# Every edge-value multiply of a two-layer GNN kernel reads its edge values from PSUM

## The chip, the cores and the metric

One NeuronCore of a Trainium2 chip runs the whole program. The metric is the device time of one execution in microseconds (us).

## The reference

Two graph layers over 6250 nodes with 96 features and 106250 edges that are sorted by destination, each followed by a residual and a layer norm:

```python
h = gelu(x @ W_pre + b_pre)
msg = h[src] * edge_attr                      # layer 0: gather, multiply
aggr = segment_sum(msg, dst)
x1 = x + aggr;  y = gelu(gelu(x1 @ W1 + b1) @ W2 + b2)
x2 = layernorm(x + (x1 + y))
deg = segment_sum(1, dst); dinv = rsqrt(max(deg, 1))
h2 = x2 @ W_lin.T + b_lin                     # layer 1
agg = segment_sum(h2[src] * dinv[src] * dinv[dst], dst)
out = layernorm(x2 + relu(agg + x2 @ W_root.T + b_root))
```

The change touches the second line only, and there the place from which VectorE reads `edge_attr`.

## The kernel before

**Units.** The edges are cut in tiles of 128 and the tiles in units of five (`UT`): units 0 to 165 are whole, unit 166 holds the last ten edges. For each unit GpSimd gathers the five tiles of `h[src]` with five indirect DMAs into one of eight slots of `gath` (L923); SP loads the edge values into one of four slots of `edg`; VectorE makes a one-hot of each edge's destination within a window of nodes (`hot`, L1352) and multiplies gath by the edge values into `msg` (`multiply`, L1376); TensorE multiplies msg by the one-hot and so sums the messages of the unit's window in the bank `seg` or `seg_odd` (L1590); VectorE adds the finished window to `sumT` (`add`, L1396). A window is 128 nodes wide up to group 21 (units 0 to 65) and 64 from there on.

**What frees what.** The gathers of unit u wait for the multiply of unit u-8, SP's load of edge values for the multiply of unit u-4. The multiply of unit u waits for its gathers and its edge values.

**The bank.** Up to `AHEAD` = 108 every even unit (`by_bank`) has its edge values copied by ScalarE from `edg` into the PSUM bank `edges_ps` (`copy_edges`, L1086), and its multiply reads the bank; the odd units, and all from 108 on, read `edg` in SBUF. The copy waits until the last multiply that read the bank is done. The bank `edges_ps` is later the third bank for sums of pieces. The bank `counters` holds `iota_ps` (0 to 127, against which every one-hot is compared) and the two iotas of the builder in bf16.

**The second layer beside the first.** Layer 1 runs as dense counts: a builder on VectorE makes one-hots for pairs of windows (L1472, L1474, four pairs in one build, 157 builds, two buffers), TensorE turns each of the 625 pairs into counts (L1622, banks `bank_q[0]` and `bank_b`), ScalarE casts them into SBUF (L1026), SP stores them to HBM and loads them back as pieces (eight buffers), and TensorE sums pieces against the ready node rows (L1646), which VectorE adds to `sumT` or `upper` (`dense`, L1499). The node steps of layer 0 (step0, 13 chunks with up to 16 phases over all engines: gelu, norm, products) are put between them.

**The order.** `schedule()` writes one list, and each engine walks it and executes its own items in that order. One slot of the list belongs to one unit: the unit itself (on VectorE one-hot and multiply, on TensorE the sums), then adds, dense sums, stores and loads, then in at least eight places the pairs, each with a piece or a step beside it where one is due. A slot up to unit 104 holds one build with four pairs or two builds with eight. The copy for unit u+1 stands at place 2 of slot u, behind two pairs. From `AHEAD` on the multiply of unit u+1 already stands in slot u (`hot` at place 3, `product` at place 5).

Of the kernel before, what the change touches and what calls it, by code (L numbers as in the profile page):

```python
# [12 lines left out]
P = 128  # L13
N_NODES, D = 6250, 96
# [5 lines left out]
UT = 5  # L20
# [3 lines left out]
UNITS = BODY_TILES // UT  # L24
# [8 lines left out]
WIN = 128  # L33
# [5 lines left out]
GS, ES, MS = 8, 4, 5  # L39
# [84 lines left out]

def group_of(u):
    return min(u // GU if u < WIDE * GU else WIDE + u - WIDE * GU, GROUPS - 1)


def by_bank(u):

    return u % 2 == 0 and u < AHEAD


def reach(g):
# [40 lines left out]
def schedule():  # L175
# [68 lines left out]
    for u in range(ALL_UNITS):  # L244
        if u < AHEAD:
            order += [("add", g) for g in range(WIDE, GROUPS) if added[g] == u]
            order.append(("unit", u))
        else:
            order.append(("sums", u))
        if u >= ALL_UNITS - GS:  # L250
            order.append(("back", u - (ALL_UNITS - GS)))
        if u == FLAG_AT:
            order.append(("flag", 0))
        order += [("add", g) for g in range(WIDE) if added[g] == u]
        flush(u)
        order += [("store", k) for k in range(STORES) if stored[k] == u]
        if u >= LOAD_AT and (u - LOAD_AT) % LOAD_STEP == 0 and (u - LOAD_AT) // LOAD_STEP < len(LOADED):
            order.append(("load", LOADED[(u - LOAD_AT) // LOAD_STEP]))
        credit += CREDIT[u > built]
        pairs = []  # L260
        for j in range(BUILDS):
            if BUILD_AT + int(j * BUILD_STEP) == u:
                order.append(("build", j))
                pairs += range(j * BP, min(j * BP + BP, PAIRS))
        slots = max(len(pairs), 2 * CT)
        for i in range(slots):
            for k, (p, c) in enumerate(steps[u]):
                if k * slots // len(steps[u]) == i:
                    order.append(("step0", p, c))
                    if p == phases_of(c)[-1]:  # L270
                        known = c + 1
            if i == 2 and u < UNITS and by_bank(u + 1):
                order.append(("edges", u + 1))
            if AHEAD <= u + 1 < ALL_UNITS:
                if i == 2:
                    order += [("add", g) for g in range(WIDE, GROUPS) if added[g] == u + 1]
                if i == 3 and u <= TOGETHER:
                    order.append(("hot", u + 1))
                elif i == 5 and u < TOGETHER:
                    order.append(("product", u + 1))  # L280
                elif i == 4 and u == TOGETHER:
                    order += [("product", u + 1), ("hot", u + 2), ("product", u + 2)]
            if i < len(pairs):
                order.append(("pair", pairs[i]))
                for k in range(STORES):
                    if last_pair_of(k) == pairs[i]:
                        stored[k] = u + 1
            if credit >= CT:
                was = len(pieces)
                if open_run or not (waiting and u <= built + 1):  # L290
                    next_piece(u, next(n for until, n in LEAST if u < until))
                if len(pieces) > was:
                    credit -= tiles_of_cut(pieces[-1][1])
                else:
                    credit = min(credit, 2.0 * CT)
# [32 lines left out]
def build(nc, x, xT_in, src, dst, first, tile_first, tile_rows, edge, edge_tail, W_pre, b_pre, W1, b1, W2, b2,  # L328
          WlinT, b_lin, WrootT, b_root, out):
    with ExitStack() as ctx:  # L330
# [252 lines left out]
        one_bank = sum(1 for r in range(len(runs)) if any(  # L583
            x[2] == r and order.index(("piece", q)) < last_pair for q, x in enumerate(pieces)))

        last_copied = max(u for u in range(UNITS) if by_bank(u))
        two_banks = sum(1 for r in range(len(runs)) if any(
            x[2] == r and order.index(("piece", q)) < sums_at(last_copied + 1) for q, x in enumerate(pieces)))

# [87 lines left out]

        def set_bank(c):
            return (bank_q[0], bank_q[1], edges_ps, seg, seg_odd, bank_a, bank_b)[c % 7]

        def group_sum(g):

# [302 lines left out]
        def _(act):  # L985
# [91 lines left out]
                        act.dma_start(rows[part], back(c)[part]).then_inc(s_out[c % ZS], 16)  # L1077

            def copy_edges(u):
                if u > 0:  # L1080
                    act.wait_ge(s_msg, u - 1)
                else:
                    act.wait_ge(s_kb, 3)
                act.wait_ge(s_edge[u % ES], edges_landed(u))
                if u < UNITS:
                    act.copy(edges_ps[:, 0:UT * D], edg[:, u % ES].rearrange("p j d -> p (j d)")).then_inc(s_eps, 1)  # L1086
                else:
                    for j, k in enumerate(TAILS):
                        last = act.copy(edges_ps[0:k, j * D:(j + 1) * D], edg[0:k, u % ES, j, :])
                    last.then_inc(s_eps, 1)  # L1090

            act.wait_ge(s_w, 8 * 16)
# [23 lines left out]
        def general_dve(dve, r, rows):  # L1116

            if r == 0:
                dve.memset(sumT[:], 0.0).then_inc(s_cleared, 1)
                dve.wait_ge(s_cleared, 1)  # L1120
                dve.wait_ge(s_const, 2)
                dve.sem_inc(s_lmsg, 1)
            dve.sem_inc(s_ladd[r], 1)

            def general_unit(g, ks):
                tiles = len(ks)
                dve.wait_ge(s_ladd[r], g * WINDOWS + 1)
                dve.tensor_copy(dst_f[:, 0:tiles], dsts[:, bass.ds(g * UT, tiles)]).then_inc(s_ldst[r], 1)
                if r == 0:
                    dve.wait_ge(s_lgath[0], g * (16 * UT) + 16 * tiles)  # L1130
                    dve.wait_ge(s_ledge, g * 16 + 16 * (tiles if ks is TAILS else 1))
                    if ks is TAILS:
                        for j, rows_j in enumerate(ks):
                            last = dve.tensor_tensor(msg[0:rows_j, 0, j, 0:D], gath[0:rows_j, j, :],
                                                     edg[0:rows_j, 0, j, :], ALU.mult)
                        last.then_inc(s_lmsg, 1)
                    else:
                        dve.tensor_tensor(msg[:, 0, 0:tiles, 0:D], gath[:, 0:tiles],
                                          edg[:, 0, 0:tiles], ALU.mult).then_inc(s_lmsg, 1)
                with dve.Fori(0, WINDOWS) as w:  # L1140
                    dve.wait_ge(s_ldst[r], g + 1)
                    dve.wait_ge(s_ladd[r], g * WINDOWS + w + 1)
                    dve.tensor_scalar(rel[:, 0:tiles], dst_f[:, 0:tiles],
                                      win_start[:, bass.ds(w, 1)], None, ALU.subtract
                                      ).then_inc(s_lrel[r], 1)
                    dve.wait_ge(s_lrel[r], g * WINDOWS + w + 1)
                    dve.tensor_tensor(
                        onehot[:, 0, 0:tiles],
                        iota_ps[:].unsqueeze(1).to_broadcast([P, tiles, WIN]),
                        rel[:, 0:tiles].unsqueeze(2).to_broadcast([P, tiles, WIN]),  # L1150
                        ALU.is_equal).then_inc(s_loh[r], 1)
                    dve.wait_ge(s_lseg[r], g * WINDOWS + w + 1)
                    dve.tensor_tensor(sumT[0:rows, bass.ds(w * WIN, WIN)],
                                      sumT[0:rows, bass.ds(w * WIN, WIN)],
                                      seg[0:rows, 0:WIN], ALU.add).then_inc(s_ladd[r], 1)

            with dve.Fori(0, UNITS) as g:
                general_unit(g, sizes(0))
            general_unit(UNITS, TAILS)
            dve.wait_ge(s_ladd[r], ALL_UNITS * WINDOWS + 1)  # L1160

# [118 lines left out]
        def _(dve):  # L1280
# [65 lines left out]
            def hot(u):  # L1346
# [3 lines left out]
                w = reach(group_of(u))  # L1350
                if u < UNITS:
                    dve.tensor_tensor(  # L1352
                        onehot[:, s, :, 0:w], iota_ps[:, 0:w].unsqueeze(1).to_broadcast([P, UT, w]),
                        rel[:, u * UT:(u + 1) * UT].unsqueeze(2).to_broadcast([P, UT, w]),
                        ALU.is_equal).then_inc(s_oh, 1)
                else:
                    for j, k in enumerate(TAILS):
                        t = u * UT + j
                        last = dve.tensor_tensor(onehot[0:k, s, j, 0:w], iota_ps[0:k, 0:w],
                                                 rel[0:k, t:t + 1].to_broadcast([k, w]), ALU.is_equal)  # L1360
                    last.then_inc(s_oh, 1)

            def multiply(u):
                s = u % MS
                if by_bank(u):
                    dve.wait_ge(s_eps, u // 2 + 1)
                    edges = by_tile(edges_ps, UT)
                else:
                    dve.wait_ge(s_edge[u % ES], edges_landed(u))
                    edges = edg[:, u % ES]  # L1370
                if u < EARLY:
                    dve.wait_ge(s_h, CHUNKS - (-(u + 1) * UT // CT))
                else:
# [453 lines left out]
```

## Time and profile before

| | us |
|---|---|
| median of 3 runs | 1125.99 (1120.19 to 1127.88) |
| the profiled execution | 1126.56 |
| its span, from the first to the last instruction | 1124.8 |
| TensorE busy | 938.3 (83%) |
| GpSimd busy | 833.6 (74%) |
| VectorE busy | 719.1 (64%) |
| ScalarE busy | 473.2 (42%) |

All times of the trace are from the start of the span. Instructions that only issue or wait aren't counted as busy; idle time before an instruction is given with what ended it. Where that is "issue", the engine waited for nothing that the profile shows. The granted clock of TensorE is a share of 2.4 GHz.

### The profile page before, as it was taken

What the parts mean: (1) busy time and instruction counts of PE and PEld (TensorE: products, weight loads), DVE (VectorE), ACT (ScalarE), POOL (GpSimd) and SP (SyncE); (2) the same over time, 40 slices, a digit from 0 to 9 for tenths busy, and PEclk for the clock granted to TensorE, in tenths of its full rate; (3) what the DMA queues carried; (4) which work ended last, traced back from release to release, by engine and by line L of the source; (5) the groups of instructions that cost most, each with busy time, mean ns of one, the idle gap of its engine ahead of it and who ended that gap; (6) DMA issues with size and microseconds to landing.
All of it is one profiled execution on the core that took longest, in us unless ns stands there. A gap on an engine that the chain in (4) does not pass through costs nothing. (4 is left out here: it accounts for less than half of the span.)

```text
span 1124.8 us, 21017 instructions
## 1 busy us (share of the span) xinstructions
PE 938.3 (83%) x7410; PEld 792.9 (70%) x7847; DVE 719.1 (64%) x1521; ACT 473.2 (42%) x884; POOL 833.6 (74%) x917
## 2 busy tenths in 40 slices
PE   5877677677767887898889889899999989889786
PEld 5844445344444775685678678799999989789786
DVE  8976797677767667756576666634336454646567
ACT  1366685665665566555565556600001010001115
POOL 7877777777777777777777777777777777777715
PEclk9997986888877999696699999999999999879898
DMA  9457776675666769777788889998999997767853
GB/s 286 111 156 251 243 227 218 225 231 173 236 212 194 241 217 300 229 239 240 251 259 262 269 292 300 282 286 251 266 269 293 266 257 217 217 167 203 206 127 90
DMA packets 185723, 260.28 MB, mean 231 GB/s; under 512 B 68651, under 2 KB 163883, under 8 KB 179019
## 3 DMA queue, kind: packets, MB, share of 16 engines
q1 hardware_dynamic: 158049, 215.51, 59.7%
q0 software_dynamic: 26992, 42.82, 16.1%
q8 instruction: 61, 1.00, 0.4%
q10 hardware_dynamic: 569, 0.53, 0.2%
q14 instruction: 52, 0.42, 0.1%
HBM read 173.15 MB, written 85.62 MB: 230 GB/s over the span
## 5 line engine op out<-in xcount | busy, mean ns | idle before, releaser
L923 POOL DMA_INDIRECT gath<-table_h,srcs x806 | 784.6, 973 | 245.6 <-issue 242.5
L1646 PE MATMUL bank_q<-piece_raw,early_late 128*96 128x250 bf16 x2805 | 339.1, 273 | 8.2 <-DVE sumT L1499 6.0
L1646 PEld LDWEIGHTS bank_q<-piece_raw,early_late 128*96 128x96 bf16 x2805 | 304.9, 124 | 2.1 <-issue 0.5
L1026 ACT CAST counts_raw<-bank_q 128x490 bf16<-128x490 f32 x300 | 185.2, 617 | 201.9 <-PE bank_q L1622 198.7
L1026 ACT CAST counts_raw<-bank_b 128x490 bf16<-128x490 f32 x300 | 186.2, 621 | 46.8 <-PE bank_b L1622 46.1
L1622 PE MATMUL bank_q<-hots_raw 128*128 128x245 bf16 x626 | 134.9, 300 | 80.2 <-ACT counts_raw L1026 55.1
L1474 DVE TENSOR_TENSOR hots_raw<-counters,kb 128x1960 bf16<-128x1960 bf16 (+1 forms) x157 | 182.5, 1163 | 0.0
L1622 PE MATMUL bank_b<-hots_raw 128*128 128x245 bf16 x624 | 134.9, 301 | 19.9 <-ACT counts_raw L1026 7.1
L1590 PE MATMUL seg<-onehot,msg 128*97 128x64 f32 (+1 forms) x830 | 111.2, 290 | 23.9 <-DVE msg L1376 23.6
L1590 PE MATMUL seg_odd<-onehot,msg 128*97 128x64 f32 (+1 forms) x832 | 108.8, 286 | 23.3 <-DVE msg L1376 22.6
L1590 PEld LDWEIGHTS seg<-onehot,msg 128*97 128x97 f32 x830 | 103.2, 193 | 33.6 <-DVE msg L1376 31.6
L1472 DVE TENSOR_TENSOR hots_raw<-counters,kb 128x1024 bf16<-128x1024 bf16 (+1 forms) x157 | 106.8, 681 | 24.8 <-PE bank_b L1622 24.8
L1590 PEld LDWEIGHTS seg_odd<-onehot,msg 128*97 128x97 f32 x832 | 101.3, 189 | 29.8 <-DVE msg L1376 27.3
L1622 PEld LDWEIGHTS bank_q<-hots_raw 128*128 128x128 bf16 x626 | 44.6, 102 | 110.2 <-ACT counts_raw L1026 99.5
L1038 ACT ACTIVATE y<-bank_a,b1c 96x512 f32<-96x512 f32 (+2 forms) x14 | 8.8, 629 | 236.3 <-PE bank_a L1661 236.2
L1376 DVE TENSOR_TENSOR msg<-gath,edg 128x480 f32<-128x480 f32 x112 | 72.8, 650 | 48.6 <-DMA gath<-table_h,srcs 48.6
L1622 PEld LDWEIGHTS bank_b<-hots_raw 128*128 128x128 bf16 x624 | 50.1, 103 | 75.7 <-ACT counts_raw L1026 68.0
L1352 DVE TENSOR_TENSOR onehot<-counters,rel 128x320 f32<-128x320 f32 (+1 forms) x166 | 102.0, 614 | 0.0
L1376 DVE TENSOR_TENSOR msg<-gath,edges_ps 128x480 f32<-128x480 f32 x54 | 35.2, 652 | 81.1 <-ACT edges_ps L1086 81.0
L1499 DVE TENSOR_TENSOR sumT<-sumT,bank_q 96x250 f32<-96x250 f32 x91 | 37.1, 409 | 70.2 <-PE bank_q L1646 66.3
L1538 PEld LDWEIGHTS <-w_pre 97*128 97x128 bf16 x437 | 45.1, 109 | 51.8 <-DVE hots_raw L1474 27.0
L1646 PE MATMUL edges_ps<-piece_raw,early_late 128*96 128x250 bf16 x648 | 79.5, 273 | 0.0
(237 smaller groups left out, 796.7 us busy)
## 6 DMA issues: line engine op xcount, KB each, us to landing
counts_hbm<-counts_raw SPq DMA_DIRECT2D x50, 1531.2 KB
piece_raw<-counts_hbm SPq DMA_DIRECT2D x250, 250.0 KB
edg<-in_edge SPq DMA_DIRECT2D x166, 240.0 KB
gath<-table_h,srcs POOLq DMA_INDIRECT x806
piece_raw<-counts_hbm SPq DMA_DIRECT2D x38, 125.0 KB
piece_raw<-counts_hbm SPq DMA_DIRECT2D x25, 187.5 KB
counts_raw<-counts_hbm SPq DMA_DIRECT2D x4, 625.0 KB, 6.5
table_h<-stage SPq DMA_DIRECT2D x12, 192.0 KB, 5.4
```

What stands on the lines that cost most here:

```text
L923: pool.indirect_dma_start(gath[0:k, u % GS * UT + j, :], None, table[0], bass.IndirectOffsetOnAxis(ap=srcs[0:k, t:t + 1], axis=0)).then_in ...
L1026: act.copy(counts[:, k % 2, :, i * WD:(i + 2) * WD].rearrange("p a (w n) -> p a w n", w=2), counted).then_inc(s_kept, 1)
L1038: act.activation(y1[0:D, 0:tiles * P], bank_a[0:D, 0:tiles * P], ACT.Gelu, bias=b1c[:, 0:1]).then_inc(s_y1, 1)
L1352: dve.tensor_tensor(onehot[:, s, :, 0:w], iota_ps[:, 0:w].unsqueeze(1).to_broadcast([P, UT, w]), rel[:, u * UT:(u + 1) * UT].unsqueeze(2). ...
L1376: dve.tensor_tensor(msg[:, s, :, 0:D], gath[:, slot_tiles(u), :], edges, ALU.mult).then_inc(s_msg, 1)
L1472: dve.tensor_tensor(hot_b(j)[:, 0:n], iota_b.unsqueeze(1).to_broadcast([P, n, P, 2]), blocks.unsqueeze(2).to_broadcast([P, n, P, 2]), ALU. ...
L1474: dve.tensor_tensor(hot_k(j)[:, 0:n], iota_k.unsqueeze(1).to_broadcast([P, n, KC, 2]), keys.unsqueeze(2).to_broadcast([P, n, KC, 2]), ALU. ...
L1499: dve.tensor_tensor(total, total, run_sum, ALU.add).then_inc(s_dense, 1)
L1538: pe.ldweights(w_pre[:].bitcast(BF16)[:, 0:P])
L1590: last = pe.matmul(group_sum(g), msg[0:k, u % MS, j, :], onehot[0:k, u % MS, j, 0:reach(g)], start=(u == first_unit(g) and j == 0), stop=( ...
L1622: last = pe.matmul(pair_bank(m)[:, w * KC:(w + 1) * KC], hot_b(j)[:, i, :, w], hot_k(j)[:, i, :, w], start=True, stop=True)
L1646: mm = pe.matmul(sums(r)[0:D, 0:DN], parts[:, FINE[c] + i, part, :], rows, start=(first and i == 0 and part == 0), stop=(last and i == til ...
```

## The change

`by_bank` is gone: every unit has its edge values copied into a bank, and every multiply reads one. Up to unit 107 that is `edges_ps`; from unit 108 on it is the bank `counters`, whose place the copies overwrite, so the one-hots of these units compare against `iota` in SBUF. The copy of unit u waits for the multiply of u-1 (before, for that of u-2), the first copy into `counters` also for all builds and for the one-hots of units 0 to 107. The copy for unit u+1 stays at place 2 of slot u.

```diff
-            if i == 2 and u < UNITS and by_bank(u + 1):
+            if i == 2 and u <= TOGETHER:
                 order.append(("edges", u + 1))
+                if u == TOGETHER:
+                    order.append(("edges", u + 2))
...
-        last_copied = max(u for u in range(UNITS) if by_bank(u))
+        last_copied = AHEAD - 1
...
+        def edges_of(u):
+            return (edges_ps if u < AHEAD else counters)[:, 0:UT * D]
+        def iota_of(u):
+            return iota_ps if u < AHEAD else iota
...
             def copy_edges(u):
-                if u > 0:
-                    act.wait_ge(s_msg, u - 1)
+                if u == 0:
+                    act.wait_ge(s_kb, 3)
+                elif u == AHEAD:
+                    act.wait_ge(s_hots, BUILDS)
+                    act.wait_ge(s_oh, AHEAD)
                 else:
-                    act.wait_ge(s_kb, 3)
+                    act.wait_ge(s_msg, u)
                 act.wait_ge(s_edge[u % ES], edges_landed(u))
                 if u < UNITS:
-                    act.copy(edges_ps[:, 0:UT * D], edg[:, u % ES].rearrange("p j d -> p (j d)")).then_inc(s_eps, 1)
+                    act.copy(edges_of(u), edg[:, u % ES].rearrange("p j d -> p (j d)")).then_inc(s_eps, 1)
...
                     dve.tensor_tensor(
-                        onehot[:, s, :, 0:w], iota_ps[:, 0:w].unsqueeze(1).to_broadcast([P, UT, w]),
+                        onehot[:, s, :, 0:w], iota_of(u)[:, 0:w].unsqueeze(1).to_broadcast([P, UT, w]),
...
             def multiply(u):
                 s = u % MS
-                if by_bank(u):
-                    dve.wait_ge(s_eps, u // 2 + 1)
-                    edges = by_tile(edges_ps, UT)
-                else:
-                    dve.wait_ge(s_edge[u % ES], edges_landed(u))
-                    edges = edg[:, u % ES]
+                dve.wait_ge(s_eps, u + 1)
+                edges = by_tile(edges_of(u), UT)
```

## Rows read from the trace of the kernel before

**Rows 1.** The page: span, and busy time of each engine.

```profile
span 1124.8 us, 21017 instructions
...
PE 938.3 (83%) x7410; PEld 792.9 (70%) x7847; DVE 719.1 (64%) x1521; ACT 473.2 (42%) x884; POOL 833.6 (74%) x917
```

**Rows 2.** Instructions by line and form: count, busy us, mean ns, idle before, releasers.

```profile
L923 POOL DMA_INDIRECT gath<-table_h,srcs x806 | 784.6, 973 | 245.6 <-issue 242.5 <-DVE msg L1376 3.1
...
L1376 DVE TENSOR_TENSOR msg<-gath,edg 128x480 f32<-128x480 f32 x112 | 72.8, 650 | 48.6 <-DMA gath<-table_h,srcs 48.6
...
L1352 DVE TENSOR_TENSOR onehot<-counters,rel 128x320 f32<-128x320 f32 x100 | 48.2, 482 | 0.0
...
L1086 ACT COPY edges_ps<-edg 128x480 f32<-128x480 f32 x54 | 31.9, 591 | 0.7 <-DVE msg L1376 0.7
```

**Rows 3.** Line 923 alone: shortest, median, longest ns; first and last start.

```profile
L923 POOL DMA_INDIRECT gath<-table_h,srcs x806: 890/944/1922, 44.8 to 1073.9; - x162
```

**Rows 4.** The chain that ended last: start us, us, what.

```profile
1040.51 5.91 DMA gath<-table_h,srcs
```

**Rows 5.** The timeline (start us, us): multiplies and the gathers beside them.

```profile
61.19 0.65 DVE L1376 TENSOR_TENSOR msg<-gath,edg 128x480 f32<-128x480 f32 x1
61.25 1.41 POOL L923 DMA_INDIRECT gath<-table_h,srcs  x1 [0.30 <-issue]
...
399.62 0.65 DVE L1376 TENSOR_TENSOR msg<-gath,edges_ps 128x480 f32<-128x480 f32 x1 [4.26 <-ACT edges_ps L1086]
399.83 0.94 POOL L923 DMA_INDIRECT gath<-table_h,srcs  x1 [0.30 <-issue]
...
702.24 0.65 DVE L1376 TENSOR_TENSOR msg<-gath,edg 128x480 f32<-128x480 f32 x1
...
702.45 1.25 POOL L923 DMA_INDIRECT gath<-table_h,srcs  x1 [0.30 <-issue]
...
1067.07 0.65 DVE L1376 TENSOR_TENSOR msg<-gath,edg 128x480 f32<-128x480 f32 x1
1067.12 1.41 POOL L923 DMA_INDIRECT gath<-table_h,srcs  x1 [0.30 <-issue]
```

**Rows 6.** Waits of the whole span: who, for whom: us in total, times, longest.

```profile
DVE msg L1376 <- ACT edges_ps L1086: 81.0, 35, 5.1
...
POOL gath L923 <- DVE msg L1376: 3.1, 10, 0.3
```

**Rows 7.** The timeline around a slot with one build and no piece.

```profile
90.60 0.59 ACT L1086 COPY edges_ps<-edg 128x480 f32<-128x480 f32 x1
...
91.23 0.66 DVE L1376 TENSOR_TENSOR msg<-gath,edges_ps 128x480 f32<-128x480 f32 x1 [3.09 <-ACT edges_ps L1086]
...
91.94 1.33 PE L1590 MATMUL seg<-onehot,msg 128*97 128x128 f32 x10 [0.76 <-DVE msg L1376]
...
93.67 0.40 PE L1622 MATMUL bank_q<-hots_raw 128*128 128x245 bf16 x2 [0.39 <-DVE hots_raw L1474]
```

**Rows 8.** The timeline around a slot with one build and three pieces.

```profile
398.96 0.63 ACT L1086 COPY edges_ps<-edg 128x480 f32<-128x480 f32 x1
...
399.19 1.45 PE L1646 MATMUL bank_q<-piece_raw,early_late 128*96 128x250 bf16 x12
...
400.70 1.25 PE L1590 MATMUL seg_odd<-onehot,msg 128*97 128x128 f32 x10
```

**Rows 9.** The timeline: the multiply of unit 55.

```profile
376.81 0.66 DVE L1376 TENSOR_TENSOR msg<-gath,edg 128x480 f32<-128x480 f32 x1 [4.67 <-DMA gath<-table_h,srcs]
```

**Rows 10.** The timeline: the multiply of unit 104, the first gather of 112.

```profile
722.60 0.66 DVE L1376 TENSOR_TENSOR msg<-gath,edges_ps 128x480 f32<-128x480 f32 x1 [0.94 <-ACT edges_ps L1086]
...
726.65 0.94 POOL L923 DMA_INDIRECT gath<-table_h,srcs  x1 [0.30 <-DVE msg L1376]
```

**Rows 11.** Busy time by stretch, with granted clock; then a wait from 970 to 1086.

```profile
504.00:560.00 56.00, 48.37 (x281) 34.89 (x294) 36.07 (x74) 30.82 (x59) 42.35 (x45) 0.66 0.78 249
...
728.00:970.00 242.00, 237.90 (x2223) 232.63 (x2315) 110.69 (x302) 16.25 (x24) 184.97 (x188) 0.99 0.91 265
...
DVE msg L1376 <- DMA gath<-table_h,srcs: 16.2, 8, 4.7
```

More of the change, by code:

```diff
@@ L126, in group_of @@
     return min(u // GU if u < WIDE * GU else WIDE + u - WIDE * GU, GROUPS - 1)
-def by_bank(u):
-    return u % 2 == 0 and u < AHEAD
 def reach(g):
@@ L1079, in copy_edges @@
             def copy_edges(u):
-                if u > 0:
-                    act.wait_ge(s_msg, u - 1)
+                if u == 0:
[3 more added lines that the diff above has]
+                    act.wait_ge(s_oh, AHEAD)
                 else:
-                    act.wait_ge(s_kb, 3)
+                    act.wait_ge(s_msg, u)
                 act.wait_ge(s_edge[u % ES], edges_landed(u))
                 if u < UNITS:
-                    act.copy(edges_ps[:, 0:UT * D], edg[:, u % ES].rearrange("p j d -> p (j d)")).then_inc(s_eps, 1)
+                    act.copy(edges_of(u), edg[:, u % ES].rearrange("p j d -> p (j d)")).then_inc(s_eps, 1)
                 else:
                     for j, k in enumerate(TAILS):
-                        last = act.copy(edges_ps[0:k, j * D:(j + 1) * D], edg[0:k, u % ES, j, :])
+                        last = act.copy(edges_of(u)[0:k, j * D:(j + 1) * D], edg[0:k, u % ES, j, :])
                     last.then_inc(s_eps, 1)
@@ L1148, in general_unit @@
                         onehot[:, 0, 0:tiles],
-                        iota_ps[:].unsqueeze(1).to_broadcast([P, tiles, WIN]),
+                        iota[:, 0:WIN].unsqueeze(1).to_broadcast([P, tiles, WIN]),
                         rel[:, 0:tiles].unsqueeze(2).to_broadcast([P, tiles, WIN]),
@@ L1358, in hot @@
                         t = u * UT + j
-                        last = dve.tensor_tensor(onehot[0:k, s, j, 0:w], iota_ps[0:k, 0:w],
+                        last = dve.tensor_tensor(onehot[0:k, s, j, 0:w], iota_of(u)[0:k, 0:w],
                                                  rel[0:k, t:t + 1].to_broadcast([k, w]), ALU.is_equal)
```

## The prediction

> **What bounds the kernel.** The page first [rows 1]: no engine is full; TensorE is the busiest at 83%. Then the groups of the engines [rows 2]: GpSimd issues 806 gathers at L923, 973 ns each, and its idle time before them is 245.6 us of "issue", 0.30 us each. So it is never off that line: 784.6 + 245.6 = 1030.2 us, from 44.8 us to its last start at 1073.9 us, of a span of 1124.8 us [rows 1, 3]. GpSimd's 74% hides this, since it counts the 0.30 us as idle. The chain that ended last agrees: one gather behind the other up to 1040.51, 5.91 us of landing, then the last sums [rows 4]. The gathers are the clock of the kernel, as long as nothing makes them wait.
>
> The median gather takes 944 ns and the longest 1922 [rows 3]; if all took 944 the line would be 784.6 - 806 x 0.944 = 23.7 us shorter. The timeline says what lengthens them [rows 5]. A multiply that reads gath and edg (both SBUF) starts at 702.24; the gather of 702.45 takes 1.25 us instead of 0.94. A multiply that reads gath and edges_ps (PSUM) starts at 399.62; the gather of 399.83, the same 0.21 us behind, takes 0.94. I went through all multiplies of that view: 51 of the 112 from SBUF lengthen a gather, by 15.1 us together (27 of the 54 before unit 108 by 8.0, 4.0 of it before unit 57; 24 of the 58 from there on by 7.0); the first is at 61.19, the last at 1067.07 [rows 5]. None of the 54 from the bank does. That fits chance: 650 ns against a gather each 1249 ns gives 0.65 x 0.65 / (2 x 1.249) = 0.17 us each. The other 8.6 us come from vector work that stays.
>
> The Trainium skill, "SBUF — State Buffer", section "SBUF: two separate sides", has this as an exclusive lock that VectorE takes with two SBUF inputs and GpSimd with its own operation; whoever is first holds it and the other waits. The trace agrees for GpSimd (0.31 us at 702.45); it doesn't show VectorE waiting, the multiplies of either kind take 0.63 to 0.66 us [rows 2, 5]. By the same rule the one-hots of the late units will lock; without it the sum below would end at 1119.4 instead of 1123.2.
>
> **What the change gives.** Before unit 108, 54 multiplies leave SBUF: 8.0 us of gathers. From unit 108 on, 58 multiplies leave it (7.0 us), but the 58 one-hots now have both inputs in SBUF. They are 482 ns for 650 [rows 2]; lengthening goes by the square, so they take back 7.0 x (482/650)^2 = 3.9 us, net 3.1. No row shows such a one-hot beside a gather: the bounds are 0 (net 7.0) and the whole 7.0 (net 0); I take 3.9. Their own durations I leave, as the multiply takes 650 ns from SBUF [rows 2] and 0.65 us from the bank (399.62). GpSimd's line alone would be 11.1 us shorter.
>
> **What it costs.** ScalarE gets 112 more copies of 591 ns [rows 2] and a tiny one for the last ten edges, and every multiply before 108 now waits for one (before, every second). ScalarE executes in order: the copy for unit u+1 stands in slot u behind the cast of its second pair, VectorE waits for it, and behind the multiply on VectorE stand adds, dense sums and the builder's one-hots, for which TensorE's next pairs wait. SP's edge load behind each multiply, and the piece loads queued behind it, move as much as the multiply; eight piece buffers cover that, so I cost them at nothing; without them TensorE would wait for a piece as long as the multiply is late, some 2 us each. That is not new: VectorE already waits 81.0 us in 35 of 54 cases [rows 6]. What counts is whether TensorE waits. In a slot with one build and no pieces it does [rows 7]: copy 90.60, multiply 91.23, TensorE idle 0.76 before the unit's matmuls and 0.39 before the next pair, together 1.15 us. In a slot with pieces it doesn't [rows 8]: copy 398.96, multiply 399.62, and the matmuls of 400.70 follow without a wait, since a piece of 1.45 us ran meanwhile. In a slot with two builds six pairs stand behind the copy; there it only delays casts, by something between 0 and its 0.59 us.
>
> So I sort the schedule's even slots, which get a copy, by that rule, in the stretch where it matters. That stretch is units 57 to 107. Up to unit 55 the multiply still waits for its gather (4.67 us at 376.81) [rows 9], so stalls are absorbed there: the single-build slots among the even ones from 44 to 54 cost nothing; further ahead, up to unit 30, the gathers are 20 us and more away from the multiplies that free their buffers, so nothing there reaches them. From 57 on the common line of pairs, units and pieces falls behind, and the gathers come up against it: gather 0 of unit 112 needs the multiply of 104, which starts at 722.60 and ends at 723.26; the gather starts at 726.65, and its releaser reads as the multiply [rows 10]. Slack 3.4 us, the least of all units (units 101 to 113: 3.4 to 7.7), from 20 to 40 us elsewhere in the first half. Waits of the gathers on multiplies sum to 3.1 us, at most 0.3 [rows 6].
>
> Even slots 58 to 106: single-build without enough pieces are 74, 78, 96, 98: 4 x 1.15 = 4.6. Five more single-build ones (70, 72, 76, 80, 104) hold three or four pieces: 0; 100 and 102 hold two: 0.1 each, guessed between. Slot 106 has no build: 0. Thirteen have two: between 0 and 0.59 each, 0.15 taken as most have pieces: 2.0. Together 6.8 us, bounds 0 and 4.6 + 13 x 0.59 + 7 x 1.15 = 20.3.
>
> **The sum.** The common line at unit 104: 4.0 earlier (gathers before 57) + 6.8 later = 2.8 later. The gathers at unit 112 can't be more than 3.4 ahead of it: 2.8 - 3.4 = 0.6 us earlier than now, not the 8.0 they saved. Then 3.1 from the later units, and about 0.4 lost at the last one (its copy, at most 0.59, between its multiply and the one before). -0.6 - 3.1 + 0.4 = -3.3 us. From unit 108 on the copies I cost at nothing: ScalarE is busy 16.25 of 242 us from 728 to 970, where TensorE is busy 237.90 [rows 11]. A copy can stand there behind a gelu that waits for TensorE, but that gelu's matmul is issued by the end of the slot before, and the unit's sums come a slot later. If that cover fails, each bare wait is 0.6 us. By then the common line is 2.8 later and the gathers 3.7 earlier: 6.5 us to be caught up; VectorE's waits on gathers after 970 are 16.2 us [rows 11], so the end still follows the gathers. The profiled execution took 1126.56 us (span 1124.8), 0.6 over the median of 1125.99; 1126.56 - 3.3 = **1123.2 us**, and I give that for the median too.
>
> **Rivals.** (a) *The whole gain arrives*: TensorE loses nothing in 57 to 107 because pieces cover all. Then -4.0 - 3.4 = -7.4 at unit 112, -3.1, +0.4: -10.1, 1116.5. For it: five even slots with no stall; against: [rows 7]. With one-hots that don't lock either, -14.0: 1112.6. (b) *Slower, the common line becomes the bound*: if all 25 copies of 58 to 106 cost the 1.15 us of [rows 7], 28.8 us: -4.0 + 28.8 - 3.4 - 3.1 + 0.4 = +18.7, 1145. It decides from 10.1 us of stalls on (that is no change) and passes 1% from 21 us. With the bound 20.3 above: 1136.8. For it: VectorE waits for the copy in 35 of 54 cases [rows 6], so its lead over ScalarE is short; against: [rows 8]. (c) *The one-hots lock like the multiplies*, 3.1 not gained: 1126.3. (d) *The bank isn't what spares the gathers*: then no gain, 6.8 - 3.4 + 0.4: 1130.4; [rows 5] speak against.
>
> **Chances.** Forecast 0.52, (a) 0.15 and 0.05 with free one-hots, (b) 0.17, (c) 0.08, (d) 0.03. About 1%, 11.3 us, is what a measurement tells from no change. Faster by that (under 1114.7) needs (a) and more: 0.12. Slower (over 1137.3): 0.12. Within: 0.76. The range holds the forecast, (a) with free one-hots and (b) up to its bound: 1112 to 1137; the forecast's own is 1118 to 1131.
>
> **What would show it.** Gathers: median still 944, the mean down from 973 to about 959. No msg<-gath,edg left; lengthened gathers from 748 on under one-hots. VectorE's wait on the copies up from 81 us; TensorE's waits on msg and hots_raw up by some 5 us in 392 to 745. New: GpSimd waits for multiplies, some 5 to 8 us around 700 to 760, where now it is 0. If there is no such wait, the limit at unit 104 was wrong and (a) holds. It would also be wrong by another granted clock: between 504 and 560 it is 0.66 now [rows 11], in the very stretch that sets the slack.

## The result, and the profile after

| | median us | runs | profiled span |
|---|---|---|---|
| before | 1122.97 | 20, 1120.19 to 1128.02 | 1124.8 |
| after | 1128.45 | 20, 1123.1 to 1134.07 | 1127.2 |
| predicted | 1123.2 | range 1112 to 1137 | |

The changed kernel is slower: ratio 1.0042, 95% interval 1.0029 to 1.0055. I had forecast 3.3 us less; by the ratio it is some 4.7 us more (the two medians lie 5.5 apart). That is inside the range and within the 1% I called no change, but the sign is wrong. The profiled execution of before (1126.56 us) lies 3.6 us above its median of 20, that of after (1129.03 us) 0.6 above; so the two spans are only 2.4 us apart, and a single profile's microseconds at the end of the line carry an error of that size.

The groups of instructions of after first (busy time, mean ns | idle before them and what ended it), each form by itself:

```profile
L928 POOL DMA_INDIRECT gath<-table_h,srcs x806 | 773.6, 960 | 262.2 <-issue 239.4 <-DVE msg L1380 22.7
L1380 DVE TENSOR_TENSOR msg<-gath,edges_ps 128x480 f32<-128x480 f32 x108 | 70.3, 651 | 166.2 <-ACT edges_ps L1094 166.0
L1094 ACT COPY counters<-edg 128x480 f32<-128x480 f32 x58 | 32.6, 562 | 171.3 <-DVE msg L1380 166.4 <-DVE onehot L1360 4.9
L1360 DVE TENSOR_TENSOR onehot<-iota,rel 128x320 f32<-128x320 f32 x58 | 28.1, 484 | 0.0
```

The gathers (L928, L923 before) took 784.6 us in [rows 2]: 11.0 us are gone, and no gather is lengthened by a multiply any more. But 22.7 us of their idle time now end with a multiply, where [rows 6] had 3.1. GpSimd's waits in one stretch of after:

```profile
core 0 of [0], span 1127.2 us
engine line waited for: us in total, times, longest us
POOL gath L928 <- DVE msg L1380: 20.0, 11, 3.0
POOL gath L928 <- issue: 19.8, 65, 0.3
```

That is 629 to 741 us: eleven gathers stand still for up to 3.0 us, 16.6 us more in all than the 0.30 each that they take anyway. So the 8 us which the gathers gained before unit 108 are lost there, and more: gather 0 of unit 112 is at 732.7, 6.0 us later than the 726.65 of [rows 10]; gather 0 of unit 96 was still 8.5 us early. The gather of unit 112 waits for the multiply of 104, which is at 731.3, 8.7 us later than the 722.60 of [rows 10]. The common line (of pairs, units and pieces, which TensorE walks) lost that time.

The other direction shows it too. In the kernel before, VectorE waits for gathers before 17 of its multiplies:

```profile
DVE msg L1376 <- DMA gath<-table_h,srcs: 48.6, 17, 5.9
```

The list of waits of after has no such line at all (the control below has 3.3 us). In the changed kernel no multiply waits for its gathers, so it is the common line and not the gathers that sets the end. Where it lost its time, a count by slot shows (a slot: from the first matmul of one unit's sums to that of the next; in brackets, how much of it TensorE is idle):

```
slot       before        after         with the copy first in 78, 96, 98
78       5.55 (0.30)   6.31 (0.85)    5.55 (0.30)
79       6.60 (0.91)   7.51 (1.49)    6.59 (0.91)
85       7.84 (0.00)   9.40 (0.00)    7.84 (0.00)
96       4.10 (0.75)   5.01 (1.50)    4.57 (1.22)
97       9.72 (0.48)  10.61 (1.12)    9.71 (0.48)
98       3.66 (0.48)   4.57 (1.23)    3.67 (0.48)
99       9.32 (0.60)  11.10 (0.60)    9.33 (0.59)
57-107 355.4 (45.4)  363.7 (50.3)    357.2 (47.6)
```

Slot 96 in after, by the timeline (start, length, engine; in brackets the idle time before and what ended it). The order of ScalarE's instructions is what counts:

```profile
start us, us, engine line op out<-in xcount [idle before <-releaser]
677.02 1.28 ACT L1043 ACT_TABLE_LOAD   x1
677.23 1.45 PE L1650 MATMUL bank_q<-piece_raw,early_late 128*96 128x250 bf16 x12
...
678.32 0.68 ACT L1043 ACTIVATE y<-bank_a,b1c 96x512 f32<-96x512 f32 x1
...
678.90 0.60 ACT L1031 CAST counts_raw<-bank_q 128x490 bf16<-128x490 f32 x1
...
679.39 0.61 ACT L1031 CAST counts_raw<-bank_b 128x490 bf16<-128x490 f32 x1
...
679.88 0.58 ACT L1094 COPY edges_ps<-edg 128x480 f32<-128x480 f32 x1
...
680.49 0.66 DVE L1380 TENSOR_TENSOR msg<-gath,edges_ps 128x480 f32<-128x480 f32 x1 [4.53 <-ACT edges_ps L1094]
...
681.20 1.07 PE L1594 MATMUL seg_odd<-onehot,msg 128*97 128x64 f32 x10 [0.75 <-DVE msg L1380]
...
681.41 0.94 POOL L928 DMA_INDIRECT gath<-table_h,srcs  x1 [1.54 <-DVE msg L1380]
...
683.24 0.12 PEld L1626 LDWEIGHTS bank_q<-hots_raw 128*128 128x128 bf16 x2
683.25 0.39 PE L1626 MATMUL bank_q<-hots_raw 128*128 128x245 bf16 x2 [0.64 <-DVE hots_raw L1478]
```

VectorE sits idle for 4.53 us, and what it waits for is the copy; the copy stands behind a gelu with its table load and two casts. When the multiply comes, everything that waited for it is late at once: unit 97's sums (0.75), a gather (1.54), and, through the builder's one-hots, the next pair (0.64). And there is a second loss, in slots 85 and 99, where TensorE is not idle more than before. The windows view (PE, PEld, DVE, ACT and POOL busy, then granted clock, DMA share, GB/s):

```profile
592.30:595.70 3.40, 3.40 (x20) 3.30 (x21) 1.43 (x5) 1.65 (x3) 2.48 (x4) 0.51 0.83 277
698.10:701.50 3.40, 3.40 (x18) 3.07 (x20) 2.45 (x5) 0.76 (x2) 2.57 (x3) 0.51 0.78 264
```

In the same slots of the kernel before:

```profile
591.00:594.40 3.40, 3.40 (x36) 3.34 (x37) 0.69 (x3) 2.15 (x4) 2.77 (x3) 1.00 0.99 294
690.60:694.00 3.40, 3.40 (x34) 3.36 (x37) 2.87 (x5) 1.44 (x3) 2.51 (x3) 1.00 1.01 284
```

Two stretches of 3.4 us at half the granted clock (the 1.2 GHz level) with TensorE busy throughout; before has 1.00 there. Slots 85 and 99 are 1.56 and 1.78 us longer for it. The kernel before has such a stretch elsewhere, at 496.0 in slots 71 and 72 (granted 0.50), and after has not: its slot 72 is 1.35 us shorter (7.90 before, 6.55 in after; 7.79 in the control, which has the stretch).

### The profile page after: what moved, and what is told of

It is laid out like the page before. It is cut to its first block and busy times, and to the rows that moved or that the text cites. A ratio compares the mean times of both kernels' runs of the same rounds, so it can differ in the third digit from the quotient of the medians.

```text
span 1127.2 us, 21243 instructions
## 1 busy us (share of the span) xinstructions
PE 935.9 (83%) x7410; PEld 786.8 (70%) x7847; DVE 720.1 (64%) x1521; ACT 527.6 (47%) x997; POOL 821.4 (73%) x917
## 5 line engine op out<-in xcount | busy, mean ns | idle before, releaser
L928 POOL DMA_INDIRECT gath<-table_h,srcs x806 | 773.6, 960 | 262.2 <-issue 239.4
L1650 PE MATMUL bank_q<-piece_raw,early_late 128*96 128x250 bf16 x2787 | 334.9, 272 | 5.6 <-DVE sumT L1503 2.3
L1650 PEld LDWEIGHTS bank_q<-piece_raw,early_late 128*96 128x96 bf16 x2787 | 301.6, 124 | 3.9 <-DMA piece_raw<-counts_hbm 1.9
L1380 DVE TENSOR_TENSOR msg<-gath,edges_ps 128x480 f32<-128x480 f32 x108 | 70.3, 651 | 166.2 <-ACT edges_ps L1094 166.0
L1094 ACT COPY counters<-edg 128x480 f32<-128x480 f32 x58 | 32.6, 562 | 171.3 <-DVE msg L1380 166.4
L1360 DVE TENSOR_TENSOR onehot<-counters,rel 128x640 f32<-128x640 f32 (+1 forms) x108 | 73.8, 683 | 0.0
L1650 PEld LDWEIGHTS edges_ps<-piece_raw,early_late 128*96 128x96 bf16 x666 | 70.3, 123 | 1.1 <-DMA piece_raw<-counts_hbm 1.1
```

The costliest lines, as they stand in the source:

```text
L928: pool.indirect_dma_start(gath[0:k, u % GS * UT + j, :], None, table[0], bass.IndirectOffsetOnAxis(ap=srcs[0:k, t:t + 1], axis=0)).then_in ...
L1094: act.copy(edges_of(u), edg[:, u % ES].rearrange("p j d -> p (j d)")).then_inc(s_eps, 1)
L1360: dve.tensor_tensor(onehot[:, s, :, 0:w], iota_of(u)[:, 0:w].unsqueeze(1).to_broadcast([P, UT, w]), rel[:, u * UT:(u + 1) * UT].unsqueeze( ...
L1380: dve.tensor_tensor(msg[:, s, :, 0:D], gath[:, slot_tiles(u), :], edges, ALU.mult).then_inc(s_msg, 1)
L1650: mm = pe.matmul(sums(r)[0:D, 0:DN], parts[:, FINE[c] + i, part, :], rows, start=(first and i == 0 and part == 0), stop=(last and i == til ...
```

## The experiments

The ratios are to the kernel before on the same chip, which is another one for each group; its median was 1123.17 us in the first group of runs (down to the copy first), 1123.91 in the second (to nine buffers) and 1123.37 in the third.

**The change once more.**

> The changed kernel itself, unaltered, on the chip of the other three, so that its own spread from one execution to the next is seen beside them. Both theories: 1.002 to 1.006 of the kernel before. The common line of pairs, units and pieces should again be about 9 us later than before at unit 104, and GpSimd should wait some 17 to 23 us for multiplies; if these two move by several us between two profiles of one kernel, single profiles may only be read for what is larger than that.

1126.72 us, ratio 1.0031 (1.0017 to 1.0045). Its profile repeats the other: gathers 773.2 us, 13.5 us of extra waits of gathers, slots 57 to 107 8.9 us longer, both half-clock stretches (589.0 and 694.8). Only unit 57 differs: its line is 3.4 us earlier than before, where in after it is 0.4 later.

**The units before 108 alone.** One-hots, and the multiplies from 108 on, as before.

```diff
-            if i == 2 and u <= TOGETHER:
+            if i == 2 and u + 1 < AHEAD:
...
-            return iota_ps if u < AHEAD else iota
+            return iota_ps
...
```

> Only the first half of the change: units 0 to 107 all read the bank edges_ps, units from 108 on multiply from SBUF and compare against the iota in PSUM as before. Theory P (place): the loss comes from the copies of the odd early units, each behind two pair casts; then the gathers at unit 112 are again about 6 us late, nothing is regained afterwards, and the whole is 5 to 8 us slower than before, 2 to 3 us slower than the full change. Rival L (late): the late copies or the one-hots against SBUF cost what the early ones gain; then this kernel is faster than before by some 4 us.

1130.72 us, 1.0058 (1.0037 to 1.0079). The gathers of unit 112 are 2.4 us late, not the 6 that I expected, since the line is 3.1 us early at unit 57 as in the control; those of unit 160 are 5.6 late.

**The units from 108 on alone.** Of the earlier ones only the even are copied, as before.

```diff
+def by_bank(u):
+    return u % 2 == 0 or u >= AHEAD
...
```

> Only the second half: even units up to 106 by the bank as before, odd ones from SBUF; all units from 108 on by the bank of the counters, their one-hots against the iota in SBUF. Theory P: the late half is a pure gain of the size of its shorter gathers, 7.0 us taken away and about 5 given back to the one-hots (5.3 us under 18 one-hots in the profile of the changed kernel): 1 to 3 us faster than before, nothing lost at unit 112. Rival L: slower than before by 2 us or more.

1121.23 us, 0.9973 (0.9957 to 0.9988), and no gather waits beyond its 0.3 us. The two parts add up: +0.58% and -0.27% make +0.31%, which is what the control shows. The late half brings what was to come of it; the loss is in the early half.

**The copy first.** The full change, with ScalarE's copy for unit u+1 at the head of slot u, ahead of the dense step and of all pairs.

```diff
         for i in range(slots):
+            if i == 0 and u <= TOGETHER:
+                order.append(("edges", u + 1))
...
-            if i == 2 and u <= TOGETHER:
-                order.append(("edges", u + 1))
...
```

> The full change, but the copy for unit u+1 stands at the head of slot u on ScalarE, ahead of the steps and of the two pairs, and not at place 2. The copies are as many and as long. Theory P: VectorE gets the next unit's edge values 0.6 us after its own multiply, its wait on the copies falls from 166 us to under 60, the common line is no later than before at unit 104, GpSimd doesn't wait, and the 11 us of shorter gathers arrive: 5 to 11 us faster than before. Rival T (time): it is the 0.59 us that each copy takes from ScalarE between casts, wherever it stands; then it stays as slow as the full change, within 2 us.

**1112.2 us, 0.9894 (0.9874 to 0.9913)**: the fastest of all. Its waits:

```profile
DVE msg L1380 <- DMA gath<-table_h,srcs: 68.8, 28, 5.5
DVE msg L1380 <- ACT edges_ps L1094: 28.3, 21, 5.1
POOL gath L928 <- DVE msg L1380: 3.4, 11, 0.3
```

166.0 us of waiting for copies became 28.3, no gather waits for a multiply beyond 0.3 us, and VectorE waits for gathers again (68.8 us, none in after): they are the bound once more. Slot 96 has the copy ahead of the table load now:

```profile
659.16 0.58 ACT L1094 COPY edges_ps<-edg 128x480 f32<-128x480 f32 x1
...
659.76 1.28 ACT L1043 ACT_TABLE_LOAD   x1
659.78 0.66 DVE L1380 TENSOR_TENSOR msg<-gath,edges_ps 128x480 f32<-128x480 f32 x1 [1.55 <-ACT edges_ps L1094]
```

The multiply comes 1.3 us after the slot's start (658.47), in after 4.3 us (680.49 against 676.19). Neither half-clock stretch is there, the line at unit 104 is 14.8 us ahead of before, the gathers 8.8 at unit 112 and 11.9 at unit 160. The gain I had predicted for the gathers is paid out in full. Slots 57 to 107 take 346.8 us for 363.7, and the clock has a share in that: the mean granted clock over them is 0.931 for 0.911, an estimated 8.5 us of the 16.9 if each us counts as lost by the part of the clock that is missing to 1.

**The copy first in the kernel before.** Is the place worth something by itself?

> The kernel before, with the banks as they are there, but its 54 copies at the head of their slots. Theory P (the gathers are the clock, the place of the copy only matters where the common line reaches them): the common line is 5 to 10 us earlier than before at unit 104, the slack of the gathers grows from 3.4 us to 8 or more, but no gather gets shorter, so the whole is within 3 us of the kernel before. Rival V: the place itself is worth the time, whatever the gathers do; then 6 us or more of the 12 that the full change with the copy first gained over before show here.

1122.89 us, 0.9991 (0.9978 to 1.0004): nothing. The line is 12.4 us earlier at unit 112, but

```profile
L923 POOL DMA_INDIRECT gath<-table_h,srcs x806 | 785.2, 974 | 245.5 <-issue 243.1
```

the gathers are as long as before, and they set the end (VectorE waits 87.5 us for them). With the banks alone the gathers are short and the line is late; with the place alone the line is early and the gathers are long. Only both together pay in full.

**The copy first from slot 57 on**, and, the other way round, **only before slot 57**.

> The full change, with the copy at the head of the slot in slots 57 and later alone; up to slot 56 at place 2. Theory W (the loss arises where I put it, from unit 57 on): the common line is earlier than before at unit 104, no or little wait of GpSimd for multiplies, and the whole is 8 to 12 us faster than before, as with the copy first everywhere. Rival E (the debts of the early slots 4 to 30 carry through): it stays 3 us or more behind the kernel with the copy first everywhere.

> The full change, with the copy at the head of the slot up to slot 56, and at place 2 from slot 57 on. Theory W: the common line is level with its gathers at unit 57 (4 to 5 us earlier than before) and still loses 8 to 9 us up to unit 104; GpSimd waits some 12 us or more; the whole is 2 to 5 us slower than before, as the full change. Rival E: 5 us or more faster than before. Two short stretches of TensorE at half its granted clock, near units 85 and 99, are there in all three kernels whose odd early units are copied at place 2 and in no other; Theory W expects them here too.

From 57 on: 1111.71 us, 0.9891 (0.9874 to 0.9908), as good as everywhere. Only before 57: 1124.41, 1.001 (0.9997 to 1.0023), less slow than I expected, with 9.1 us of extra waits of six gathers at 674 to 733 us and both half-clock stretches (584.8 and 690.7); the line is 6.0 us early at unit 64 and 1.6 late at 112. So the loss is in slots 57 to 107, as the prediction placed it; the earlier slots seem to be worth 2 us as long as the later ones stay wrong (1.001 for the 1.0031 of the control, and these intervals overlap).

**Nine gather buffers** (`GS` 8 to 9) instead of another place, so that a gather waits for the multiply of nine units back.

> The full change with nine unit buffers for the gathers (GS 9 for 8), so that a gather waits for the multiply of nine units before and not of eight. Stalls and copies stay as they are. Theory G (the loss reaches the end only through the gathers' wait for their buffers): one more unit is 6.3 us of slack; the wait of 13 to 17 us falls to about 7 to 11, and the whole comes out 3 to 6 us faster than the full change, at or below the kernel before. Rival C (the common line itself sets the end): no more than 1 us faster than the full change.

1125.34 us, 1.001 (0.9994 to 1.0025). The gathers of unit 104 are 9.4 us early (in after 1.7), yet those of 112 only 1.0, and the extra waits are still 10.4 us: the line is 7.9 us late at 104, and the buffer covers that in part. I had expected 3 to 6 us less than the full change; it is 1.4 less than the control, and the intervals overlap. The gathers of unit 160 are 4.0 us earlier than in the control, and VectorE waits for none of them in the whole span. So this run speaks for the rival: more slack lets the gathers come earlier, but the common line sets the end, and it loses the same time (slots 57 to 107 take 364.7 us), at a clock that falls in the same two places.

**The copy first in slots 78, 96 and 98 alone.**

```diff
+AT_HEAD = (78, 96, 98)
+            if i == 0 and u in AT_HEAD:
+                order.append(("edges", u + 1))
...
```

> The full change with the copy at the head of the slot in slots 78, 96 and 98 alone, and where the change has it in all others. In the profiles of the change those three slots hold 2.1 us more of TensorE's idle time than before. If the loss sits in a few slots as I reckoned in the prediction, the line at unit 104 is earlier by 2 to 5 us and the time is 1122 to 1125 us (the change ran at 1126.7 and 1128.5 us), and the short stretch at half the granted clock near 697 us, which follows slots 96 to 98, is gone while that near 591 us stays. If the loss is spread over all slots from 57 to 107, nothing moves: 1126 to 1129 us.

1120.81 us, 0.9974 (0.9959 to 0.9988): three of 108 places take back 5.9 us of the control's time, more than the 2 to 5 that I expected. The table above has its slots. 78, 79, 97 and 98 are at the length they had before, and both half-clock stretches are gone, not only the one near 697 that I expected, though slot 84, which lies just before slot 85, idles 1.51 us as in after. Slot 85 of this kernel:

```profile
589.00:592.40 3.40, 3.40 (x35) 3.34 (x36) 1.17 (x4) 1.99 (x4) 2.68 (x3) 1.00 0.83 237
```

Up to slot 77 the order of this kernel is that of after, so the first stretch followed from what slot 78's copy does to slots 78 and 79, which end 40 us ahead of it. Whether it is their 1.1 us of idle time or the 1.7 us by which all that follows comes later, no run tells apart, and of this kernel there is one profile. Slots 57 to 107 are 6.5 us shorter than in after, the line at 104 is 0.6 us ahead of before, the extra waits of the gathers fall from 16.6 to 7.3 us. I had expected 2 to 5 us at the line; against the control it is 6.1. I counted the stalls alone.

**The odd units from 59 to 107 uncopied**, all others by the bank.

```diff
+    return u < 58 or u % 2 == 0 or u >= AHEAD
...
```

> The full change, but the odd units from 59 to 107 read their edge values from SBUF again, uncopied, as before the change; all others by the bank. The theory says that this takes the loss away (25 copies behind pieces in the slots where TensorE is full) and gives back only the half of the early locks that lie there, some 4 us of the gathers' lengthening: gathers near 777 us, GpSimd's waits for the multiply under 3 us, no stretches at half clock near 590 and 697 us, a time of 1116 to 1120 us. If the odd units' copies after slot 57 are not the cause, the time is that of the change with 4 us of longer gathers on top, 1126 to 1131 us.

1118.82 us, 0.9958 (0.9944 to 0.9972). Slots 57 to 107 take 355.5 us, as before the change (355.4), without the half-clock stretches of slots 85 and 99, 1.0 us of extra waits; 11 gathers lengthened by 3.4 us are the price. This undoes just the 25 copies in question, and 7.9 us come back although the gathers get longer.

**Each early copy made twice**, at the head of the slot. Is it ScalarE's own time that costs?

```diff
+                    if u < AHEAD:
+                        act.copy(edges_of(u), edg[:, u % ES].rearrange("p j d -> p (j d)")).then_inc(s_eps, 1)
+                        act.wait_ge(s_eps, 2 * u + 1)
...
```

> The kernel with the copies first (1112.2 us), with each of the 108 early copies made twice, the second after the first is complete, so ScalarE has some 0.7 us more work per unit, about 70 us in all, at the head of the slot. The theory that the loss came from where the copy stood (behind matrix pieces, with the multiply and so the gathers waiting for it, and TensorE then short of ScalarE's evictions) says that the copy's own length at the head matters little: 1112 to 1117 us. The rival, ScalarE's time itself (each copy delays its evictions and TensorE behind them, wherever it stands), says that half of the 50 odd and even copies' 35 us from slot 57 on reach the common line: 1125 us or more, units 104 to 112 later by 10 us.

1114.22 us, 0.9918 (0.9904 to 0.9933). The windows view for 392 to 728 us, first of this kernel, then of the one with single copies (the fourth figure of busy time is ScalarE's):

```profile
392.00:728.00 336.00, 291.22 (x2363) 244.07 (x2477) 219.75 (x421) 236.25 (x432) 254.44 (x268) 0.93 0.84 265
```

```profile
392.00:728.00 336.00, 293.50 (x2379) 247.32 (x2489) 219.76 (x422) 206.79 (x379) 254.29 (x269) 0.93 0.83 268
```

29.5 us more of ScalarE's work in that stretch moved the line by 4.3 us (10.5 early at unit 104 instead of 14.8) and the time by 2.0 (the intervals of the two ratios overlap). The rival, 1125 us or more, is out: the copy's place costs, hardly its length.

**The counters' iota kept in PSUM, the sums on two banks to the end**, with the copy first. The copies go to `edges_ps` for all units, so it can't become the third bank of the sums, and the late one-hots can't lengthen a gather.

```diff
-            return (r - one_bank) % 2 if r < two_banks else (r - two_banks) % 3
+            return (r - one_bank) % 2
...
-            return (edges_ps if u < AHEAD else counters)[:, 0:UT * D]
+            return edges_ps[:, 0:UT * D]
...
-            return iota_ps if u < AHEAD else iota
+            return iota_ps
...
```

> All copies at the head of their slot, as in the kernel with the copies first (1112.2 us, gathers 772.4 us), but the edge values stay in their own bank to the end and the one-hots' counters stay in PSUM, so the sums alternate between two banks to the end instead of using three from unit 108 on. The theory that a gather is lengthened by any VectorE instruction with two inputs in SBUF says that the 18 gathers which one-hots lengthened by 4.8 us are whole again: gathers near 768 us, a time of 1107 to 1110 us. The rival says that from unit 108 on the third bank of the sums is worth more than that (the dense work is then the bound): TensorE's idle time after 728 us grows and the time is 1112 us or more, though the gathers are as short as that. A second rival says the gathers stop mattering once 11.9 us are left of their lengthening: gathers shorter, time the same 1112 us.

1116.64 us, 0.9938 (0.9924 to 0.9952): 4.4 us slower than with one-hots that lengthen gathers, though

```profile
L928 POOL DMA_INDIRECT gath<-table_h,srcs x806 | 767.4, 952 | 245.5 <-issue 243.1
```

the gathers are 5.0 us shorter, none lengthened by a one-hot, and 16.4 us early at unit 160. The line is only 10.1 early there. So the gathers no longer set the end; shortening them further buys nothing. The time expected was 1107 to 1110 us; its first rival has it: the third bank is worth more. TensorE's pieces wait for VectorE's additions to free a bank, first in this kernel, then in the one with three banks:

```profile
PE bank_q L1647 <- DVE sumT L1500: 11.1, 6, 3.1
```

```profile
PE bank_q L1650 <- DVE sumT L1503: 4.3, 2, 2.6
```

All these waits lie from 1010 us on, and units 160 to 164 take 35.3 us of the common line for 32.1. That is 3.2 of the 5.3 us between the two profiled spans. The other part isn't explained: the line is 2.6 us behind at unit 104 already (and 4.5 at unit 57), where both programs do the same.

## Why the prediction was wrong, point by point

**The bound: right for the kernel before, wrong for the changed one.** Before, and with the place alone, VectorE waits for gathers (48.6 and 87.5 us), and an earlier line gains nothing. In after it waits for none; and the chain that ended last runs over gathers from 972 us on in the kernel before, over none in after. "So the end still follows the gathers" was the step that failed here: of the 16.2 us of [rows 11], which were to keep the end with the gathers, 0.0 are left in after and 1.7 in the control.

**The gathers' own gain: right.** The bank spares them: the time beyond 806 x 0.944 us was 23.7 and became 12.7, 11.0 less for the 11.1 that I had reckoned. [rows 5] were enough for that.

**The one-hots: somewhat too low.** 18 of the 58 lengthen a gather, by 5.3 us (15 to 19 of them, 4.3 to 5.1 us, in the other profiles with such one-hots), for 3.9 in the sum. One of them, in after:

```profile
766.73 0.48 DVE L1360 TENSOR_TENSOR onehot<-iota,rel 128x320 f32<-128x320 f32 x1
766.88 1.15 POOL L928 DMA_INDIRECT gath<-table_h,srcs  x1 [0.30 <-issue]
```

The rule of the Trainium skill, "SBUF — State Buffer", "SBUF: two separate sides", foretold this, and the trace agrees on GpSimd's side (1.15 us for 0.94); VectorE's one-hots stay at 484 ns on the mean, where they had 482. This gather ends 0.82 us behind the one-hot, that of 702.45 in [rows 5] 0.81 us behind its multiply, so of its 0.94 us alone some 0.12 run beside the VectorE instruction. The other possibility of the sum, one-hots that lock nothing, is out.

**"4.0 earlier at unit 57": mis-sized by up to 4.** Measured: 0.4 later in after, 3.4 earlier in the control, 3.1, 2.4 and 1.6 in the three other kernels whose order up to there is the same. I had said that stalls up to 55 cost nothing because the multiplies wait for their gathers there. They delay the line by 8.8 us at unit 24, and then nothing waits for a gather any more: VectorE's waits for gathers up to unit 56 were 32.4 us before and are 0.0 in after, 1.6 in the control. So shorter gathers could not bring the line forward at unit 57; that took the copies first in the early slots (5.2 us earlier at unit 57 in two profiles, 2.5 and 0.7 in two others). The pairs and pieces of the first half also run at a clock that is at half in other places of each profile (0.85 on the mean from 56 to 392 us in after, 0.88 in the control), and the five profiles of one order of work differ by 3.8 us. A term of which I had one profile deserved bounds.

**The stalls of 57 to 107: 6.8 reckoned, 8.3 measured (8.9 in the control).** This term failed in two ways, and with the one above it makes the common line at unit 104 8.7 us later (5.5 in the control), where I had 2.8: the step that turned the sign. The slots were nearly the right ones: 78, 96 and 98 (74 shows nothing). But one stall of 1.15 us per slot was the wrong form. The late multiply of slot u delays that slot's end by 0.76 to 0.91, and in slot 79 and slot 97, each two builds, the pairs behind it are late again, 0.91 and 0.89. The sum, 4.4 us for my 4.6, is near by luck. What the sum lacked is the clock: TensorE's work falls to half the clock for 3.4 us later on, twice, 3.3 us in all, in slots 85 and 99, which are no more idle than before. I had named another granted clock as a way to be wrong, but only for 504 to 560, and at no price. The double builds and the rest came to about 0.6 net, not 2.0 (slots 62, 71, 76 and 84 up 0.2 to 0.5 each, 72 and 80 down by 1.4 and 0.5; that of 72 is the clock too, the stretch at 496.0 that after lacks).

**The slack of 3.4 at unit 104: nearly right.** The line 8.7 late gave gathers 6.0 late, in the control 5.5 gave 2.8, with the early units alone 5.0 gave 2.4, so the slack is 2.6 to 2.7 and every microsecond of the line reaches the gathers of unit 112. Of the 5.9 us between 2.8 and 8.7, 4.4 are the start at unit 57 and 1.5 the slots. But these late gathers are a mark of the late line, not the way by which it reaches the end: after 112 no multiply waits for them. The line itself is 8.7 late at unit 112 and 8.4 at 144. It makes good 5.7 us up to unit 165, since before waits there for its gathers and after doesn't, and ends 2.7 late, for 2.4 us of profiled span.

**After 112: 3.1 reckoned, 2.6 to 3.0 measured.** By so much the gathers of units 112 to 165 are shorter (262.3 and 261.9 us for 264.9). The size is right, within what such a reading can tell: with the early units alone, where nothing from 108 on was changed, they take 266.9. But in after the end doesn't follow the gathers. With the late units alone the gathers of unit 160 are 3.8 us early and the time 2.7 us less.

**The rivals.** (b) is what happened: the common line became the bound, at less than the 10.1 us of stalls from which I said that it decides. By the measured start (0.4 late, not 4.0 early) my own sum has it decide from 5.7, and 8.3 were there. (a) was priced at 1116.5; with the copy first its condition holds, and the time is lower still (1112.2). (c) would have been 1126.3 and (d) 1130.4, near what was measured, but for other reasons: no gather is lengthened under a multiply. A time near a rival's is no proof of it. And I had taken the copy's place in its queue as given; that it could stand ahead of two casts, at no cost that shows, was the question behind the case.

## What to carry to other kernels

Where work of a second engine is put into a chain, look first at what stands ahead of it in that engine's queue: here a copy of 0.59 us cost up to 4.5 us of waiting behind a gelu and two casts, and put first it could be made twice for 2 us. A gain on the line that sets the end is paid out only while that line still sets it: look in the changed kernel for who waits for whom, not only at which line is how late. And a few slots can hold much of a loss (three of 108 were worth 5.9 of the 14.5 us between the control and the copy first): count by slot before costing all at one price.

## What the runs showed that I had not expected

Short stalls of TensorE can be paid for twice. In all five profiles with the odd units' copies behind a pair in slots 78 and 96 to 98 (four kernels and the control) there are two stretches of 3.4 us at half the granted clock (0.51), in slots 84 and 85 and in slot 99, with TensorE busy throughout. In none of the nine others, the kernel before among them, are they there, though three of these have a like stretch near 496 us, as two of the five have. Putting one copy first took away 1.1 us of idle time in slots 78 and 79, and with it the first stretch, which begins 40 us after they end, and 1.56 us. And VectorE's one-hots with both inputs in SBUF lengthen gathers just as the multiplies did: 18 of 58, by 5.3 us together or 0.29 each, where 51 of 112 multiplies had done it by 15.1, 0.30 each.
